# Ten propagation steps on TensorE: adjacency as weights, or y as weights

## The chip, the cores and the metric

The kernel runs on one core of a Trainium2 chip. The metric is the device time in microseconds (us) of one execution, from the first to the last instruction. Engines: PE (TensorE), DVE (VectorE), ACT (ScalarE), POOL (GpSimd), SP (SyncE, which here only issues DMAs).

## The reference

A graph network with four layers over 6250 nodes of 128 features and 100,000 edges, sorted by destination. Only the last layer is touched. It is a propagation over ten steps:

```python
norm = deg_inv_sqrt[src] * deg_inv_sqrt[dst]
def step(xk, _):
    msg = norm[:, None] * xk[src]
    agg = jax.ops.segment_sum(msg, dst, num_segments=n_nodes)
    return ((1.0 - ALPHA) * agg + ALPHA * h, None)
xK, _ = jax.lax.scan(step, x, None, length=10)
```

A step needs the whole result of the step before it: each node sums the rows of its sources.

## The kernel before

Nodes are padded to NT = 49 tiles of 128. In layer 3 the state C (f32) is kept in SBUF, scaled by the degrees, and called y. Each step sums y over the edges, for two kinds of destination tile:

- **Dense tiles**, the first DENSE = 38. Layer 0 has made the adjacency as a matrix of fp8 counts in DRAM (`adj`). A row of tiles of it, 128 partitions of 6272 bytes (784 KB), is loaded for each destination tile into one of six slots of `adj_ring` (`load_adj`, issued by SP once the tile that used the slot is multiplied).
- **Pooled tiles**, the last POOLED = 11. POOL gathers the y rows of their edges from DRAM, one indirect DMA per 128 edges (L988; 178 of them a step, in EGROUPS = 45 groups of up to EG = 4, in a ring `y_rows` of ERING = 5 groups); DVE makes one-hot rows (`step_hot`, L2793), and PE multiplies them (L1951).

y is held as two f16 halves side by side, an upper part and the rest (`halves(A)` in one step, `halves(E)` in the next, 256 columns per source tile). For a dense destination tile PE runs 49 matmuls (L1933): the weights are the 128x128 block of the adjacency, what moves is 128x256, both halves of one source tile. The sum of 49 stands in one of six PSUM banks, upper half in columns 0 to 127 and lower in 128 to 255, with destination nodes on the partitions.

DVE then works the tile off in four instructions: `w0` = C*sc_a + B (L2804, does not need the sum), `w1` = bank upper*sc_b + w0 (L2810), C = bank lower*sc_b + w1 (L2813, "y_tiles"), and after ACT has written the new upper half (L1416, "upper") the new lower half (L2821, "lower"). SP stores each tile's new y to DRAM (L733), into `table` or `x_spill` by turns, since POOL's gathers of the next step read it there. POOL starts a step's gathers only when all stores of the step before have landed ("y_out"), and each group only when PE is done with the group five before it ("edge_used").

Order: `step_plan` is one list, dense tile 0, 1, 2 and so on, with edge groups put between dense tiles so that they end with the last one: 45 groups among 38 tiles. `done_order` is the order in which tiles come out, and all engines follow it. The first dense tile of a step takes its 49 source tiles in `done_order` and waits for the last ones in stages (`LATE`). `settle` adds one semaphore instruction behind a wait. The ten steps are written as five calls of `two_steps`.

Of the kernel before, what the change touches and what calls it, by code (L numbers as in the profile page):

```python
# [15 lines left out]
P = 128  # L16
N_NODES, N_EDGES, D = 6250, 100000, 128
NT = (N_NODES + P - 1) // P
# [21 lines left out]
ADJ_SLOTS = 6  # L40
# [4 lines left out]
ADJ_PITCH = 1 << 13  # L45
SCALE = 1024.0
# [39 lines left out]
def build(nc, t, out):  # L86
    ctx = ExitStack()
    with ctx:
# [3 lines left out]
        def dram(name, shape, dt=F32):  # L92
# [7 lines left out]
                      "adj_in4": "dst_in0", "edge_hot0": "filter", "edge_used0": "filter_ps", "edge_rows0": "rows_in", "edge_rows1": "keys_in", "adj_in5": "y_stored", "y_out0": "spilled", "y_upper0": "seeds_in", "y_out1": "gat_back", "edge_used": "as_kept", "edge_hot_made": "x_free", "part_done": "step_link",  # L100
# [73 lines left out]
        adj_ring = arena[:, 0:ADJ_SLOTS * NP // 4].bitcast(F8).rearrange("p (s f) -> p s f", s=ADJ_SLOTS)  # L174
# [68 lines left out]

        y_rows = arena[:, ADJ_SLOTS * NP // 4:ADJ_SLOTS * NP // 4 + EG * ERING * D].rearrange("p (g k f) -> p g k f", k=EG, f=D)

# [27 lines left out]
        iota_y = w_gat[:, :].bitcast(BF16)  # L273
        bn_st, bn = sb("bn_st", [P, 14, 6]), sb("bn", [P, 4])
# [65 lines left out]
        step_plan, done_order = [], []  # L340
        for j in range(DENSE):
            step_plan.append(("dense", j))
            done_order.append(j)
            upto = min(EDGE_TILES, EG * (max(0, j - 1) * EGROUPS // (DENSE - 2)))
            for x in range(sum(kind == "edge" for kind, _ in step_plan), upto):
                step_plan.append(("edge", x))
                for i in range(DENSE, NT):
                    if near_last[i] == edge_first + x:
                        done_order.append(i)
        place = {i: p for p, i in enumerate(done_order)}  # L350

        LATE = {0: NT - 8, NT - 8: NT - 4, NT - 4: NT - 2, NT - 2: NT - 1, NT - 1: NT}
# [20 lines left out]
        def group_place(g):  # L373
            seen = 0
            for kind, x in step_plan:
                if kind == "edge" and x == g * EG:
                    return seen
                seen += kind == "dense" or any(near_last[i] == edge_first + x for i in range(DENSE, NT))

        hot_at = {}  # L380
        for g in range(EGROUPS):
            hot_at.setdefault(max(0, group_place(g) - 2), []).append(g)
        adj_loads = [len(range(u, DENSE, ADJ_SLOTS)) for u in range(ADJ_SLOTS)]
# [14 lines left out]
        step_banks = [ps[0][:, :], ps[1][:, :], ps[2][:, :], ps[3][:, :], pt[0][:, 0:512], pt[0][:, 512:1024]]  # L398
# [4 lines left out]

        def bank_of(i):
            return step_banks[i % ADJ_SLOTS] if i < DENSE else edge_banks[i % 2]
# [98 lines left out]
        def _(sp):  # L504
# [202 lines left out]
            def after_l2(b):  # L707
                if b == 0:
                    adj_r = adj.rearrange("(j p) b -> p j b", p=P)
                    ring_u8 = adj_ring.bitcast(U8)  # L710

                    def load_adj(u, j):
                        sp.dma_start(ring_u8[:, u:u + 1, :], adj_r[:, bass.ds(j, 1), 0:NP]).then_inc(sem(f"adj_in{u}"), 16)
                    sp.wait_ge(sem("ff2_ps"), ff_done[b > 0])
                    for u in range(ADJ_SLOTS):
                        load_adj(u, u)
# [6 lines left out]
                    def two_steps(pairs, last):  # L723
                        for half in range(2):
                            final = last and half == 1
                            to_v, new = ((spill_v, table_v)[half], nodes((A, E)[half]))

                            def keep_tile(p):
                                sp.wait_ge(sem("lower"), pairs * (2 * NT) + (half * NT + NT + p + 1))
                                settle(sp)  # L730
                                i = done_order[p]
                                if not final:
                                    sp.dma_start(to_v[:, i, :], new[:, i, :]).then_inc(sem(f"y_out{1 - half}"), 16)  # L733
                                elif i < FULL_TILES:
                                    sp.dma_start(out_v[:, i, :], nodes(X)[:, i, :]).then_inc(sem("out_stored"), 16)
                                else:
                                    sp.dma_start(out[i * P:N_NODES, :], nodes(X)[0:N_NODES - i * P, i, :]
                                                 ).then_inc(sem("out_stored"), 16)

                            for p, i in enumerate(done_order):  # L740
                                if i < (DENSE - ADJ_SLOTS if final else DENSE):
                                    sp.wait_ge(sem("multiplied"), pairs * (2 * NT) + (half * NT + p + 1))
                                    settle(sp)
                                    u = i % ADJ_SLOTS
                                    load_adj(u, i + ADJ_SLOTS if i + ADJ_SLOTS < DENSE else u)
                                if p:
                                    keep_tile(p - 1)
                            keep_tile(NT - 1)
# [2269 lines left out]
```

## Time and profile before

| | us |
|---|---|
| median of 3 runs | 6619.98 |
| lowest, highest | 6592.85, 6634.28 |
| span of the profiled execution | 6586.7 |
| PE busy in it | 4728.4 (72%) |
| POOL busy | 3399.2 (52%) |
| DVE busy | 2861.5 (43%) |
| ACT busy | 960.6 (15%) |

The profiled execution is 33 us under the median. Busy shares are averages over all layers; layer 3 is read in a stretch of its own. Matmuls overlap, so a busy PE is not one at its peak: the distance between starts says more. "Issue" is idle time for which the profile shows nothing that was waited for.

### The profile page before, as it was taken

The numbers are of one execution on the slowest core, as the hardware profiler recorded it, in microseconds if no ns is written. First come the engines' busy times: TensorE is split into PE (matmuls) and PEld (weight loads), VectorE is DVE, ScalarE is ACT, GpSimd is POOL, SyncE is SP. The second block draws the span as 40 slices with busy tenths as digits, with TensorE's granted clock in tenths as the row PEclk, the third lists the DMA queues.
The fourth block names the chain that finished last, engine by engine and source line by source line (L and its number), as shares of the span: only waits on it lengthen the run. The fifth ranks groups of instructions, "written<-read, shape, count | busy, mean of one in ns | idle before, by whom it ended". The sixth has DMA issues, their size and how long they took to land.

```text
span 6586.7 us, 89829 instructions
## 1 busy us (share of the span) xinstructions
PE 4728.4 (72%) x32959; PEld 3792.3 (58%) x32959; DVE 2861.5 (43%) x9191; ACT 960.6 (15%) x2766; POOL 3399.2 (52%) x3566
## 2 busy tenths in 40 slices
PE   3767468888762445555557888788888888888888
PEld 2655356555552344444445767667666666666666
DVE  6867434444433555555673323233333333233323
ACT  4656311111110000012130000000000000000000
POOL 3332456666545555555514555555555555555555
PEclk8888679898885666677778989899888898888989
DMA  5222212222212222222214444444444444444444
GB/s 129 79 80 72 77 51 56 56 56 56 55 44 71 68 70 74 74 68 64 69 48 148 152 142 150 144 145 154 145 148 145 148 150 149 144 149 145 153 144 124
DMA packets 366969, 690.33 MB, mean 105 GB/s; under 512 B 101617, under 2 KB 247703, under 8 KB 366512
## 3 DMA queue, kind: packets, MB, share of 16 engines
q1 hardware_dynamic: 246948, 445.91, 21.7%
q0 software_dynamic: 113216, 235.39, 13.8%
q8 instruction: 271, 4.44, 0.3%
q10 hardware_dynamic: 6364, 3.20, 0.2%
q14 instruction: 170, 1.39, 0.1%
HBM read 603.02 MB, written 81.51 MB: 104 GB/s over the span
## 4 chain that ended last, share of the span: by engine, by line
PE 51%; DVE 17%; another core or an unknown queue 16%; issue 12%; ACT 3%; DMA 0%; SPq 0%; POOL 0%; DVEq 0%; ACTq 0%
PE ps L1933 24%; PE pt L1933 11%; PE ps L1674 5%; PE pt L1951 4%; DVE E L2374 3%; DVE B L2454 2%; DVE arena L2496 1%; PE pt L2018 1%; DVE O L2937 1%; PE pt L1642 1%; PE ps L2009 1%; PE ps L1751 1%; ACT E L1484 1%; DVE scores L2933 1%
## 5 line engine op out<-in xcount | busy, mean ns | idle before, releaser
L988 POOL DMA_INDIRECT arena<-table,src_i x890 | 848.6, 953 | 824.2 <-PE pt L1951 293.7
L988 POOL DMA_INDIRECT arena<-x_spill,src_i x890 | 848.8, 954 | 699.8 <-PE pt L1951 273.7
L953 POOL DMA_INDIRECT E<-gat_table,src_i x782 | 760.2, 972 | 632.2 <-DVE arena L2496 364.9
L938 POOL DMA_INDIRECT arena<-table,src_i x782 | 742.9, 950 | 602.7 <-issue 217.4
L1674 PE MATMUL ps<-E,arena 128*128 128x352 f32 (+22 forms) x2932 | 788.7, 423 | 274.3 <-DVE E L2374 218.0
L1933 PE MATMUL ps<-E,arena 128*128 128x256 f16 x6370 | 822.7, 287 | 195.6 <-issue 163.6
L1933 PE MATMUL ps<-A,arena 128*128 128x256 f16 x6370 | 820.9, 286 | 163.6 <-issue 160.7
L1933 PEld LDWEIGHTS ps<-E,arena 128*128 128x128 fp8e4 x6370 | 647.2, 102 | 353.2 <-issue 255.1
L1933 PEld LDWEIGHTS ps<-A,arena 128*128 128x128 fp8e4 x6370 | 644.2, 102 | 318.3 <-issue 223.1
L1674 PEld LDWEIGHTS ps<-E,arena 128*128 128x128 f32 x2932 | 518.4, 212 | 476.4 <-DVE E L2374 259.4
L2810 DVE SCALAR_TENSOR_TENSOR O<-ps,sc_b,O 128x128 f32<-128x128 f32 x260 | 91.2, 351 | 1336.8 <-PE ps L1933 628.2
L1751 PE MATMUL ps<-arena,B 128*128 128x144 f32 x2244 | 510.4, 375 | 63.8 <-issue 63.3
L2374 DVE SCALAR_TENSOR_TENSOR E<-arena,pt 128x512 f32<-128x512 bf16 (+5 forms) x782 | 480.0, 674 | 161.0 <-remote 74.6
L1751 PEld LDWEIGHTS ps<-arena,B 128*128 128x128 f32 x2244 | 412.9, 249 | 80.7 <-issue 77.8
L1933 PE MATMUL pt<-E,arena 128*128 128x256 f16 x2940 | 363.2, 280 | 62.9 <-issue 62.1
L1933 PE MATMUL pt<-A,arena 128*128 128x256 f16 x2940 | 363.5, 281 | 54.5 <-issue 53.7
L1023 POOL DMA_INDIRECT A<-first_rows,src_i x178 | 178.5, 1003 | 357.0 <-PE pt L1993 253.8
L1933 PEld LDWEIGHTS pt<-E,arena 128*128 128x128 fp8e4 x2940 | 291.6, 100 | 122.0 <-issue 83.9
L1933 PEld LDWEIGHTS pt<-A,arena 128*128 128x128 fp8e4 x2940 | 293.9, 101 | 114.1 <-issue 74.2
L2018 PE MATMUL pt<-arena,E 128*128 128x258 f16 x1862 | 306.0, 287 | 63.6 <-ACT E L1484 38.6
L2810 DVE SCALAR_TENSOR_TENSOR O<-pt,sc_b,O 128x128 f32<-128x128 f32 x230 | 80.7, 351 | 589.4 <-PE pt L1933 316.3
L1484 ACT ACTIVATE E<-ps 128x490 fp8e4<-128x490 f32 (+1 forms) x494 | 291.2, 597 | 215.5 <-remote 141.7
(353 smaller groups left out, 5601.5 us busy)
## 6 DMA issues: line engine op xcount, KB each, us to landing
arena<-adj SPq DMA_DIRECT2D x380, 784.0 KB
adj<-E SPq DMA_DIRECT2D x38, 784.0 KB
arena<-table,src_i POOLq DMA_INDIRECT x1672
O<-dst_rows SPq DMA_DIRECT2D x112, 224.0 KB
x_spill<-A SPq DMA_DIRECT2D x245, 64.0 KB
arena<-x_spill,src_i POOLq DMA_INDIRECT x890
table<-E SPq DMA_DIRECT2D x196, 64.0 KB
E<-gat_table,src_i POOLq DMA_INDIRECT x782
```

The source lines that it names most:

```text
L938: pool.indirect_dma_start(out=rows_ring[:, k % RING, :], out_offset=None, in_=table, in_offset=bass.IndirectOffsetOnAxis(ap=src_i[:, k:k + ...
L953: pool.indirect_dma_start(out=att_rows[:, b % 3 * AB + at, :], out_offset=None, in_=gat_table, in_offset=bass.IndirectOffsetOnAxis(ap=src_ ...
L988: pool.indirect_dma_start(out=y_rows[:, g % ERING, k, :], out_offset=None, in_=(table, x_spill)[half], in_offset=bass.IndirectOffsetOnAxis ...
L1023: pool.indirect_dma_start(out=rows0[:, x % (2 * EG0), :], out_offset=None, in_=first_rows, in_offset=bass.IndirectOffsetOnAxis(ap=src_i[:, ...
L1484: act.activation(made[:, i % MADE, :, 2 * BD * q:2 * BD * q + w], ps[pair % 4][:, 0:w * NT].rearrange("p (d j) -> p j d", j=NT), ACT.Copy, ...
L1674: mm = pe.matmul(ps[m % 4][:, (lo - WD * m) * BASES:(hi - WD * m) * BASES], rows_ring[:, k % RING, :], m_ring[:, k % MS, lo - first_dst(k) ...
L1751: mm = pe.matmul(ps[i % 2][:, 0:WL2], edge_hot[:, (2 * b + half) % 3, k % AH, i % 2 * P:(i % 2 + 1) * P], weighted_rows[:, b % 2, k, :], s ...
L1933: mm = pe.matmul(bank_of(x)[:, 0:2 * D], adj_ring[:, u, i * P:(i + 1) * P], y[:, i, :], start=(p == 0), stop=(p == NT - 1))
L1951: mm = pe.matmul(bank_of(i)[:, 0:2 * D], step_hot[g % EHOT][:, k, i % 2 * P:(i % 2 + 1) * P], y_rows[:, g % ERING, k, :].bitcast(F16), sta ...
L2018: mm = pe.matmul(bank0_of(m)[:, 0:2 * LO], made[:, m % MADE, j, :], y16[:, j, :], start=(j == 0), stop=(j == NT - 1))
L2374: dve.scalar_tensor_tensor(m_ring[:, k % MS, w, :], bc(iota_h[:, w], BASES), dst_rel[:, k:k + 1], row_bc(made_c[:, c % 2, at, :], w.stop - ...
L2810: dve.scalar_tensor_tensor(w1, bank[:, 0:D], sc_b[:, tile:tile + 1], w0, MUL, ADD).then_inc(part_done, 1)
```

## The change

Layer 3 is turned around. The halves of y are the weights now, each 128x128 f16, and the adjacency moves: rows of one source tile for CHUNK = 4 destination tiles at once, 128x512 fp8 (the last chunk has 2 tiles). 38 dense tiles make ten chunks. Both halves of a source tile add into the same sum, so one bank holds four tiles, but with features on the partitions and nodes in the columns. ACT copies the bank to SBUF (`sums_in`), PE turns each tile back with a transpose (`turn_banks`), and DVE then needs one read of PSUM per dense tile, not two. Pooled tiles are computed as before.

The adjacency comes in pieces, four destination rows by 17 or 16 source tiles (rows of 2176 or 2048 bytes), thirty a step, in four slots. The plan of all ten steps is one sorted list: every dense matmul pair has a cost of two units (a full chunk 98, a step `LONG` = 931), a chunk's transposes come 10 units behind its end, its store 26 units; edge group g stands at 64 + 20 g, so the last of the 45 stands 13 units into the next step. Waits are on constants; the settles are gone except on POOL.

The diff, cut:

```diff
-ADJ_SLOTS = 6
+CHUNK, PARTS3, ADJ_RING = 4, [(0, 17), (17, 33), (33, 49)], 4
+PIECE = 17
+CHUNKS = (DENSE + CHUNK - 1) // CHUNK
+TURN_LAG, STORE_LAG, EDGE_LAG, EDGE_GAP = 10, 26, 64, 20
...
+        plan = []
+        for step in range(STEPS):
+            base = step * LONG
+            for c in range(CHUNKS):
+                for i in range(NT):
+                    plan.append((base + chunk_at_cost(c) + 2 * i * len(chunk_nodes(c)) / CHUNK, 0, "dense", step, c, i))
+                plan.append((base + chunk_at_cost(c + 1), -1, "copy", step, c, 0))
+                plan.append((base + chunk_at_cost(c + 1) + TURN_LAG, 1, "turn", step, c, 0))
+                plan.append((base + chunk_at_cost(c + 1) + STORE_LAG, 4, "store", step, c * CHUNK, chunk_nodes(c).stop))
+            for g in range(EGROUPS):
+                plan.append((base + EDGE_LAG + EDGE_GAP * g, 2, "edges", step, g, 0))
+                plan.append((base + EDGE_LAG + EDGE_GAP * g - 5 * EDGE_GAP // 2, 5, "hots", step, g, 0))
+            for i in range(DENSE, NT):
+                plan.append((base + EDGE_LAG + EDGE_GAP * pooled_group(i), 3, "pooled", step, i, 0))
+                plan.append((base + EDGE_LAG + EDGE_GAP * pooled_group(i) + STORE_LAG - TURN_LAG, 4, "store", step, i, i + 1))
+        plan = [entry[2:] for entry in sorted(plan, key=lambda entry: entry[:2])]
...
+        READ_UPTO = {0: 32, 32: 36, 36: NT - 1, NT - 1: NT}
...
# SP
-                        sp.dma_start(ring_u8[:, u:u + 1, :], adj_r[:, bass.ds(j, 1), 0:NP]).then_inc(sem(f"adj_in{u}"), 16)
+                        sp.dma_start(ring_u8[:, n % ADJ_RING, 0:len(some), 0:(last - first) * P],
+                                     adj_r[:, some.start:some.stop, first * P:last * P]
+                                     ).then_inc(sem(f"adj_in{n % ADJ_RING}"), 16)
...
# ACT
+                        if kind == "copy":
+                            n, w = step * CHUNKS + what, len(chunk_nodes(what)) * P
+                            act.wait_ge(sem("chunk_made"), n + 1)
+                            if n >= 2:
+                                act.wait_ge(sem("turned_out"), n - 1)
+                            act.activation(sums_in[:, n % 2, 0:w], chunk_banks[n % 2][:, 0:w], ACT.Copy
+                                           ).then_inc(sem("turn_in"), 1)
...
# PE
-                                        mm = pe.matmul(bank_of(x)[:, 0:2 * D], adj_ring[:, u, i * P:(i + 1) * P],
-                                                       y[:, i, :], start=(p == 0), stop=(p == NT - 1))
+                            for h in range(2):
+                                mm = pe.matmul(chunk_banks[n % 2][:, 0:len(some) * P], y[:, i, h * D:(h + 1) * D],
+                                               adj_ring[:, piece % ADJ_RING, 0:len(some), at:at + P],
+                                               start=(i == 0 and h == 0), stop=(i == NT - 1 and h == 1))
...
+                            for k in range(len(chunk_nodes(what))):
+                                mm = pe.transpose(turn_banks[n % 2][:, k * P:(k + 1) * P],
+                                                  sums_in[:, n % 2, k * P:(k + 1) * P], ident[:, :])
+                            mm.then_inc(sem("turned_out"), 1)
...
# DVE
+                            for k, i in enumerate(chunk_nodes(what)):
+                                kept_of(k, i)
+                            dve.wait_ge(part_done, parts[0])
+                            dve.wait_ge(sem("turned_out"), n + 1)
+                            for k, i in enumerate(chunk_nodes(what)):
+                                dve.scalar_tensor_tensor(nodes(C)[:, i, :], turn_banks[n % 2][:, k * P:(k + 1) * P],
+                                                         sc_b[:, i:i + 1], kept_part[:, k, :], MUL, ADD
+                                                         ).then_inc(sem("y_tiles"), 1)
+                            for i in chunk_nodes(what):
+                                lower_of(step, i)
```

## Rows read from the trace of the kernel before

**Rows 1.** The page's slices: PE busy in tenths, and GB/s, 40 equal slices.

```profile
PE   3767468888762445555557888788888888888888
GB/s 129 79 80 72 77 51 56 56 56 56 55 44 71 68 70 74 74 68 64 69 48 148 152 142 150 144 145 154 145 148 145 148 150 149 144 149 145 153 144 124
```

**Rows 2.** Stretches: busy us (instructions) of each engine, clock, DMA share, GB/s.

```profile
4101.40:4410.70 309.30, 258.30 (x2100) 210.22 (x2099) 97.34 (x374) 15.15 (x49) 169.47 (x178) 0.91 0.48 148
5340.00:5650.00 310.00, 260.69 (x2096) 211.26 (x2094) 97.21 (x374) 15.15 (x49) 169.96 (x178) 0.89 0.48 148
```

**Rows 3.** Groups of one step, 4101.4 to 4410.7 (busy, mean | idle before, releasers).

```profile
L1933 PE MATMUL ps<-E,arena 128*128 128x256 f16 x1274 | 164.2, 286 | 36.9 <-issue 36.4
L1933 PE MATMUL pt<-E,arena 128*128 128x256 f16 x588 | 70.1, 277 | 7.3 <-issue 6.9
L1951 PE MATMUL pt<-arena,rows 128*128 128x256 f16 x150 | 22.4, 286 | 5.3 <-issue 5.3
L1951 PE MATMUL pt<-arena,weight_e 128*128 128x256 f16 x44 | 6.9, 272 | 1.6 <-issue 1.6
L1951 PE MATMUL pt<-arena,rel_i 128*128 128x256 f16 x44 | 6.6, 273 | 0.0
...
L2810 DVE SCALAR_TENSOR_TENSOR O<-ps,sc_b,O 128x128 f32<-128x128 f32 x26 | 9.1, 351 | 140.9 <-remote 69.4 <-PE ps L1933 60.4 <-PE pt L1951 11.1
```

**Rows 4.** Timeline of PE and its loads over one dense tile (start, us).

```profile
4404.61 5.34 PEld L1933 LDWEIGHTS ps<-E,arena 128*128 128x128 fp8e4 x49
4404.72 5.51 PE L1933 MATMUL ps<-E,arena 128*128 128x256 f16 x49
...
4410.07 0.60 PE L1951 MATMUL pt<-arena,weight_e 128*128 128x256 f16 x4
```

**Rows 5.** Stretches in runs of POOL's gathers (columns as rows 2).

```profile
4108.20:4115.80 7.60, 7.60 (x72) 6.83 (x70) 1.57 (x7) 0.00 (x0) 5.76 (x6) 1.00 0.40 140
4116.00:4133.10 17.10, 4.82 (x17) 1.46 (x15) 1.61 (x7) 0.31 (x1) 13.06 (x14) 0.64 0.37 105
...
4145.70:4152.30 6.60, 6.60 (x63) 5.93 (x61) 2.78 (x12) 0.03 (x1) 3.91 (x4) 1.00 0.50 166
4158.90:4166.40 7.50, 7.50 (x71) 6.74 (x69) 1.21 (x5) 0.31 (x1) 5.68 (x6) 1.00 0.52 155
...
4262.30:4274.30 12.00, 6.12 (x31) 3.21 (x30) 1.66 (x7) 0.31 (x1) 5.68 (x6) 0.71 0.33 86
```

**Rows 6.** Timeline of POOL (start, us; in brackets the idle time before).

```profile
4132.08 0.95 POOL L988 DMA_INDIRECT arena<-table,src_i  x1 [0.30 <-issue]
...
4158.97 0.95 POOL L988 DMA_INDIRECT arena<-table,src_i  x1 [1.82 <-PE pt L1951]
...
4167.73 0.94 POOL L988 DMA_INDIRECT arena<-table,src_i  x1 [0.30 <-issue]
```

**Rows 7.** Timeline of PE where it comes back to full pace.

```profile
4136.58 0.61 PE L1951 MATMUL pt<-arena,rows 128*128 128x256 f16 x2 [0.30 <-issue]
...
4170.43 2.12 PE L1933 MATMUL ps<-E,arena 128*128 128x256 f16 x18 [0.48 <-issue]
```

**Rows 8.** A stretch of layer 2 with fourteen gathers (columns as rows 2).

```profile
2490.60:2508.20 17.60, 11.36 (x72) 10.26 (x72) 10.62 (x28) 0.00 (x0) 13.40 (x14) 0.75 0.36 93
```

**Rows 9.** Timeline of PE in that stretch.

```profile
2501.24 0.42 PE L1817 MATMUL pt<-ident,E 128*128 128x128 f32 x1
2501.45 0.42 PE L1818 MATMUL pt<-ident,E 128*128 128x128 f32 x1
...
2506.21 0.28 PE L1751 MATMUL ps<-arena,B 128*128 128x144 f32 x1 [1.51 <-issue]
```

**Rows 10.** A group of the page: ACT reading PSUM.

```profile
L1484 ACT ACTIVATE E<-ps 128x490 fp8e4<-128x490 f32 (+1 forms) x494 | 291.2, 597 | 215.5 <-remote 141.7
```

**Rows 11.** Timeline at a step's end: last edge products, first gather.

```profile
4410.51 0.38 PE L1951 MATMUL pt<-arena,rows 128*128 128x256 f16 x2
...
4417.32 0.95 POOL L988 DMA_INDIRECT arena<-x_spill,src_i  x1 [22.69 <-DMA x_spill<-A]
```

## What the change should do to the time

> **What bounds the kernel now.** I read the slices of the page first. Layer 3 is the stretch from slice 21 on, where DMA moves 142 to 154 GB/s, and it takes nearly half of the span. PE is busy in 7 to 8 tenths there [rows 1]. A table by step then shows ten equal steps: one takes 309.3 us, with some 2,100 matmuls, 178 gathers on POOL and a granted clock of 0.91 [rows 2]. Then the groups of that step. DVE's idle time is ended by PE or a remote queue, so PE sets the pace; the reader should see that what ends PE's own idle time is "issue", 36.4 + 6.9 + 5.3 + 1.6 = 50 us of it [rows 3]. PE waits for no data that the profile knows. It runs 38 x 49 = 1862 dense matmuls and, by the same rows, 238 edge ones (two of them the next step's: 2098 in all).
>
> What would the step be without these holes? A dense tile with none has its 49 matmuls between 4404.72 and 4410.07: 109.2 ns for 256 columns [rows 4]. 2098 x 0.1092 = 229.1 us. The step is 309.3, so 80 us are lost. Where? The holes have a pattern that is best seen by laying POOL's timeline beside PE's:
> - From 4108.2 to 4133.0 POOL issues 20 gathers. PE runs 72 matmuls and 70 loads in the first 7.6 us, and then 17 matmuls and 15 loads in the next 17.1 us [rows 5]. POOL's last gather of this run ends at 4133.0 [rows 6], and PE is back at 4136.6, 3.6 us later [rows 7].
> - From 4145.7 four gathers and a pause of 1.8 us: 63 matmuls in 6.6 us, nothing lost [rows 5].
> - From 4158.97 eight gathers, 1.25 us apart, to 4168.7 [rows 6]: 71 matmuls in 7.5 us [rows 5], then a hole, and PE is back at 4170.4 [rows 7], 1.7 us after the last gather: 4 us. The run of twelve from 4254.8 leaves 31 matmuls in the 12 us from 4262.3 [rows 5]: 9 us lost.
>
> So while POOL gathers without a pause, PE is fed from a store that holds so much, and is refilled at 32 instructions in 17.1 us, 1.9 per us. The store is 142 - 7.6 x 1.9 = 128 instructions. Is it a count or a time (7.6 us)? Layer 2 tells: there PE is slower (72 matmuls in 17.6 us, [rows 8]), and 14 gathers from 2490.7 open no hole before 2504.7, 14 us in, after about 70 matmuls [rows 9]. It is a count: 140 - 14 x 1.9 = 113 instructions by this row.
>
> In the step this makes one hole of 20 us, some seven of 4 us and two or three of 9 us, less the matmuls done in them: 65 us. The other 15 us are matmuls at the lower level of the clock, 1.2 instead of 2.4 GHz, which follows the long holes: the clock stands at 0.64 and 0.71 in these, against 1.00 in whole stretches [rows 5].
>
> **The change part by part.**
> *Dense matmuls.* 1862 of 256 columns become 2 x 49 x 10 = 980: 882 of 512 columns and 98 of 256. The columns are the same 476,672. By the 109.2 ns of [rows 4], 256 columns at 2.4 GHz are 106.7 and 2.5 is left for each instruction, so 512 cost 215.8 ns: 882 x 0.2158 + 98 x 0.1092 = 201.0 us, against 203.3 now. Halving the weight loads gives nothing by itself: a load of 98 ns lies beside every one of those matmuls, and the 109.2 ns hold no room for it [rows 4]. No row shows fp8 as the moving operand; bounds are 201 and, if the columns went at the clock's lower level, 402; I take 201, since in the rows 128x256 f16 goes at a column per cycle.
>
> The Trainium skill, "TensorE: Matmul & The Clock Gate", LDWEIGHTS section, puts a load at its columns over 1.2 (107 ns) and Part 3 says that one overlaps a running matmul only if its row group differs. By that rule 882 loads saved would be worth 94 us a step. The trace disagrees: a pair takes 109.2 ns in all.
>
> *Edges:* the same 236, 25.8 us. *Transposes back:* 38 a step, f32, ident as partner. Two such transposes start 0.21 us apart [rows 9]: 8.0 us, new on PE. PE unbroken: 201.0 + 25.8 + 8.0 = 234.8 us, 6 more than now.
> *ACT:* ten copies of 128x512 at about 0.6 us (one of 490 columns: 0.6, [rows 10]) and the 49 activations: 21 us, hidden. *DVE:* one read of PSUM fewer for 38 tiles, -13 us (38 x 0.351, [rows 3]) of 97; hidden. If the chain turn, copy, DVE came late, PE has two chunk banks, 21 us each; no cost.
> *The adjacency loads:* 30 of 1.1 MB for 38 of 784 KB, rows of 2176 bytes for 6272, four slots. A piece is used in 34 x 0.216 = 7.3 us and asked for three pieces, 22 us, ahead; DMA's share is 0.48 now [rows 2]. With three times the packets the share is bounded by 0.48 and, should time go by packets, 1.4. Layer 2, whose gathers move short rows, has 93 GB/s at a share of 0.36, 258 at a full one, against 308 here [rows 2, 8]; so I take 0.6. Cost 0. SP is in order: a store waiting for "lower" holds the next load by 6 us at most, inside the 22.
> *The settles* (one semaphore instruction behind a wait on PE and SP) go. Nothing: at full pace PE shows no hole where they stand.
> *Instructions of PE:* 2 x (980 + 236 + 38) = 2508 a step for 4196.
>
> *The gathers* stay: 178 x 1.25 = 222.6 us of POOL, 5.0 us per group of four [rows 6]. But their place against PE changes, and this decides. Now a group comes between dense tiles of 5.35 us, mostly one, so that POOL pauses 1.8 us after four gathers. The new plan has a group every 20 units: 20 x 0.2158, 5.3 edge matmuls and 0.9 transposes are 5.07 us, as long as the gathers themselves, and a released POOL starts 0.9 us late, so it never pauses by itself. PE takes 52 instructions in 5.07 us, 10.3 per us, so the store shrinks at 8.4 per us and lasts 128 / 8.4 = 15.2 us (13.4 by layer 2's 113), twice as long as now.
>
> One step, from its first dense matmul:
> 1. The last group stands 13 units into the step. From PE's last edge product to POOL's first gather are 6.6 us now (4410.7 to 4417.3, [rows 11]). POOL starts at 9, group 0 has landed at 16.2 where PE wants it at 14.5: 2 us lost.
> 2. PE does groups 0, 1, 2 by 26.4, and the store is empty there. The ring holds five groups ahead, so POOL runs eight groups, until 49, and PE is back after about 54.5 (the delay after the last gather grows with the run: 1.7 us at 8, 3.6 at 20; I take 5.5 at 32). In 28 us PE does 27 matmuls at 17.1/17 us each, 5.4 us of work. Lost so far: 54.5 - 30 = 24.5 us, against 18 for the same hole now.
> 3. Now the ring is full. PE's groups x, +5.07, +10.1 and +15.2 release POOL, which starts at x + 0.9 and ends at x + 20.9; the store is empty at x + 16.1; PE is back at x + 23.8 with 7 matmuls done and does the next group at x + 26.6. Four groups in 26.6 for 20.3 us: 1.6 us lost per group. With the smaller store only three groups fit: 18.2 for 15.2, 1.0 per group. Mean 1.3, from group 3 to 39: 36 x 1.3 = 47 us (36 to 57). Then POOL is done with the step and PE runs free.
> 4. Lower clock: 15 us now. Holes fewer but longer: 15 again, 5 to 28 as bounds.
>
> Sum: 234.8 + 24.5 + 47 + 15 = 321 us a step, against 309.3: +12 a step, +120 in ten. The profiled execution's span is 6586.7 us, the median of the three runs 33 above it, so 6707 by the span and 6740 as a median. What surrounds layer 3 stays.
>
> **The rivals.**
> - *A count that just shrinks (faster).* The holes go with PE's instructions: 65 x 2508/4196 = 39 us, the clock's 15 to 9, 234.8 + 39 + 9 = 283 a step: 6350 as median. For it: the store is a count, and each instruction works twice as long. Against: POOL's pauses are gone. It decides from the point where POOL pauses 0.8 us or more about every third group, which irregular edge groups could give.
> - *No holes at all.* If 15 us of store always meet a pause, PE takes 234.8 + 2, and POOL 222.6 + 9: 240 a step, 5920. Nothing but that store speaks for it; the first run of gathers alone speaks against.
> - *The store is a time, not a count (slower).* Then PE starves 7.6 us into any run: 27.5 us in the first hole, two groups in 13.4 for 10.1 us after that, 38 x 1.65 = 63; 234.8 + 27.5 + 63 + 15 = 340, 6920. Layer 2 speaks against it [rows 8, 9]. The Trainium skill, "Runtime: NRT & Kernel Launch", Instruction fetch mechanics, has each engine's instructions streamed in 16 KiB blocks, mostly hidden, so that their number would not matter and this rival would stand; the trace has holes that it does not explain.
> - *The loads come late.* If 2176-byte rows take the packets' time of 6272, PE waits for adjacency: up to 340, 6920.
> - *The turn pays on loads:* 94 us less than now, 224, stopped by POOL at 232: 5840. [rows 4] exclude it nearly.
>
> **How the numbers follow.** Forecast 0.48, its own range 6600 to 6880; the shrinking count 0.26; no holes 0.08, with the loads' gain 0.01; time 0.08; late loads 0.09. Faster by over 1%, about what a measurement of this kernel can tell, is a step under 303: the second, third and last cases and little of the forecast's (its low end is 300): 0.37. Within 1%, 303 to 317: 0.38 of the forecast's, 0.18. Slower: 0.45. The range reaches from 6300, which takes the shrinking count in, to 6900.
>
> **What would show it.** Dense matmuls 216 ns apart in whole stretches (else the 201 is wrong); "issue" still the one reason of PE's idle time, 45 to 80 us a step; holes that open some 70 matmuls after POOL's start and close 2 to 4 us after its last gather; POOL in runs of 30 or more at the step's start and 12 to 16 after, not 4. Idle time put down to DMA would be the late loads; a step with no holes breaks the forecast.

## The result, and the profile after

| us | before | after |
|---|---|---|
| median of 4 runs | 6609.43 | 6390.7 |
| lowest, highest | 6592.85, 6634.28 | 6368.28, 6407.98 |
| span of the profiled execution | 6586.7 | 6377.2 |

The ratio is 0.9678, with an interval of [0.9634, 0.9723]: 3.2% faster. The forecast was 6740, 1.8% slower. The time lies in the range, but on the other side of no change.

The slices of the page of after: PE busy and the granted clock in tenths, and GB/s. They answer to [rows 1].

```profile
PE   3756568888874444455545888898988788798888
PEclk9878788888886666667767999899999899899999
GB/s 133 77 66 77 78 55 53 53 57 55 56 58 59 66 71 69 64 74 65 70 70 60 155 156 164 150 172 151 161 161 163 153 154 166 149 165 152 164 157 141
```

Stretches of three whole steps of after (start and end in us, length, then busy us and instructions of PE, PEld, DVE, ACT and POOL, granted clock, DMA share, GB/s). They answer to [rows 2].

```profile
4072.60:4357.20 284.60, 243.75 (x1257) 125.88 (x1255) 78.81 (x336) 19.54 (x59) 170.99 (x178) 0.93 0.52 160
4357.20:4642.40 285.20, 243.70 (x1256) 125.41 (x1254) 78.46 (x336) 19.42 (x59) 172.25 (x178) 0.94 0.52 160
5221.60:5509.40 287.80, 245.91 (x1256) 125.38 (x1254) 78.56 (x336) 19.54 (x59) 172.34 (x178) 0.92 0.51 158
```

A step takes 284.6 us where it took 309.3. The mean over the ten is 286.6 for 310.1: layer 3 gains 235 us in the profiled execution, and so holds all of the gain (its span is 209.5 shorter; layer 3 starts at 3502.5 us for 3477.2, and in the runs e4 to e8 between 3470 and 3507). PE has 1,257 matmuls for 2,100, DVE 78.8 us for 97.3, POOL its 178 gathers as before, and the DMA share went from 0.48 to 0.52 only.

Groups of PE in the step from 4072.6 (busy, mean ns | idle before, and what ended it), and its timeline in a whole stretch (start, us, operation, count):

```profile
L1950 PE MATMUL ps<-arena,E 128*128 128x512 fp8e4 (+1 forms) x980 | 218.8, 376 | 8.2 <-issue 8.1
L1962 PE MATMUL ps<-ident,O 128*128 128x128 f32 x38 | 7.3, 324 | 31.3 <-ACT O L1438 25.8 <-issue 5.5
...
3712.07 0.60 PE L1962 MATMUL ps<-ident,O 128*128 128x128 f32 x4
3712.50 1.89 PE L1950 MATMUL ps<-arena,E 128*128 128x512 fp8e4 x8
3714.99 4.48 PE L1950 MATMUL ps<-arena,E 128*128 128x512 fp8e4 x20
3719.31 0.93 PE L1980 MATMUL pt<-arena,rows 128*128 128x256 f16 x7
```

At full pace 20 dense matmuls take 4.32 us (3714.99 to 3719.31), 216.0 ns each for 512 columns, and four transposes 0.43 us. New is an idle time that ACT's copy ends: 25.8 us at L1962.

### The profile page after: what moved, and what is told of

Read it like the earlier page. It is cut to its first block, busy times and chain, and to the rows that moved or that the text cites. A ratio compares the mean times of both kernels' runs of the same rounds, so it can differ in the third digit from the quotient of the medians.

```text
span 6377.2 us, 70089 instructions
## 1 busy us (share of the span) xinstructions
PE 4557.4 (71%) x24519; PEld 2925.3 (46%) x24519; DVE 2668.5 (42%) x8811; ACT 1003.7 (16%) x2866; POOL 3558.0 (56%) x3566
## 3 DMA queue, kind: packets, MB, share of 16 engines
q0 software_dynamic: 113216, 235.39, 14.3%
## 4 chain that ended last, share of the span: by engine, by line
PE 42%; another core or an unknown queue 27%; DVE 18%; issue 10%; ACT 2%; POOL 1%; DMA 0%; ACTq 0%; DVEq 0%; SPq 0%
PE ps L1950 25%; PE ps L1697 5%; PE pt L1980 3%; DVE E L2399 3%; DVE B L2479 2%; PE pt L2043 2%; PE ps L1774 2%; DVE arena L2521 1%; PE pt L1665 1%; DVE O L2975 1%; PE ps L2034 1%; PE ps L1962 1%; POOL A L1038 1%; DVE arena L2502 1%
## 5 line engine op out<-in xcount | busy, mean ns | idle before, releaser
L1950 PE MATMUL ps<-arena,E 128*128 128x512 fp8e4 (+1 forms) x4900 | 1101.9, 377 | 84.7 <-issue 53.4
L1950 PE MATMUL ps<-arena,A 128*128 128x512 fp8e4 (+1 forms) x4900 | 1102.2, 377 | 48.3 <-issue 46.2
L1950 PEld LDWEIGHTS ps<-arena,E 128*128 128x128 f16 x4900 | 486.5, 100 | 599.6 <-issue 156.6
L1950 PEld LDWEIGHTS ps<-arena,A 128*128 128x128 f16 x4900 | 486.8, 100 | 560.8 <-issue 116.8
L2847 DVE SCALAR_TENSOR_TENSOR C<-ps,sc_b,scores 128x128 f32<-128x128 f32 x380 | 107.5, 345 | 920.6 <-PE ps L1962 656.5
L1038 POOL DMA_INDIRECT A<-first_rows,src_i x178 | 312.7, 1757 | 258.6 <-PE pt L2018 155.8
L2860 DVE SCALAR_TENSOR_TENSOR scores<-pt,sc_b,scores 128x128 f32<-128x128 f32 x110 | 38.6, 351 | 711.5 <-remote 480.9
L2975 DVE TENSOR_SCALAR O<-arena 128x245 bf16<-128x245 bf16 x988 | 231.6, 317 | 175.0 <-issue 64.4
L1962 PE MATMUL ps<-ident,O 128*128 128x128 f32 x380 | 69.6, 311 | 281.7 <-ACT O L1438 257.6
L2034 PE MATMUL ps<-O,scores 128*128 128x245 bf16 x988 | 197.2, 283 | 94.3 <-ACT E L1507 73.3
```

The source lines that it names most:

```text
L1038: pool.indirect_dma_start(out=rows0[:, x % (2 * EG0), :], out_offset=None, in_=first_rows, in_offset=bass.IndirectOffsetOnAxis(ap=src_i[:, ...
L1950: mm = pe.matmul(chunk_banks[n % 2][:, 0:len(some) * P], y[:, i, h * D:(h + 1) * D], adj_ring[:, piece % ADJ_RING, 0:len(some), at:at + P] ...
L2034: pe.matmul(ps[pair % 4][:, h * BW:(h + 1) * BW], hot_src[:, g % SRC, :], hot_code[:, g % HOT, 0:BW], start=True, stop=True).then_inc(sem( ...
L2975: dve.tensor_scalar(hot_code[:, g % HOT, 0:BW], iota_w[:, 0:BW], slot_c[:, g // P, g % P:g % P + 1], None, ALU.is_equal).then_inc(sem("hot ...
```

## Where a step's time is

By those paces PE's unbroken work is 201 (dense) + 25.8 (edges) + 38 x 0.108 = 4.1 (transposes) = 231 us. The other 53.6 of the 284.6 are 1.2 us at the start (PE waits for the first gathered rows), one long hole of 22.1, and 30.3 in the rest of the step. The hole, from both engines' timelines:

```profile
4072.59 2.75 PE L1950 MATMUL ps<-arena,E 128*128 128x512 fp8e4 x12
4081.25 0.99 POOL L1003 DMA_INDIRECT arena<-table,src_i  x1 [23.46 <-DMA table<-E]
4087.66 0.61 PE L1980 MATMUL pt<-arena,rows 128*128 128x256 f16 x4 [0.22 <-DMA arena<-table,src_i]
4093.64 4.48 PE L1950 MATMUL ps<-arena,E 128*128 128x512 fp8e4 x20
4097.96 0.60 PE L1980 MATMUL pt<-arena,rel_i 128*128 128x256 f16 x4
4099.57 0.38 PE L1950 MATMUL ps<-arena,E 128*128 128x512 fp8e4 x1 [0.33 <-issue]
...
4115.12 0.95 POOL L1003 DMA_INDIRECT arena<-table,src_i  x1 [0.30 <-issue]
4120.62 0.36 SPq L734 DMA_DIRECT2D arena<-adj  x1
4120.62 0.60 ACT L1438 ACTIVATE O<-ps 128x512 f32<-128x512 f32 x1 [42.15 <-remote]
4121.27 1.11 PE L1962 MATMUL ps<-ident,O 128*128 128x128 f32 x4 [21.32 <-ACT O L1438]
4121.50 0.95 POOL L1003 DMA_INDIRECT arena<-table,src_i  x1 [5.43 <-remote]
```

Chunk 0's last matmul ran at 4096.0. Three engines wait on what PE counted up around then: ACT for its copy, SP for the next load, POOL for the group of 4098. All three go on between 4120.6 and 4121.5, some 4.5 us after the last of 28 gathers ends (4116.1). So the semaphores that PE raises while POOL gathers without a pause arrive up to 24 us late. PE then waits for ACT's copy, which puts "ACT" where "issue" stood before; the late semaphore and the stop of PE come in the same stretch (whether the wait for ACT costs anything of its own is tested by e8).

The holes after that are small. Stretches of after, each run of twelve gathers followed by its pause:

```profile
4099.90:4121.20 21.30, 0.06 (x1) 0.00 (x0) 0.00 (x0) 0.58 (x1) 12.29 (x13) 0.54 0.16 43
...
4271.70:4286.00 14.30, 14.30 (x75) 7.17 (x74) 5.56 (x26) 0.97 (x4) 10.95 (x12) 1.00 0.69 217
4286.00:4289.40 3.40, 2.00 (x10) 0.74 (x8) 0.73 (x4) 0.54 (x1) 0.53 (x1) 1.00 0.13 34
4289.40:4304.30 14.90, 14.90 (x82) 7.91 (x80) 4.83 (x20) 1.15 (x5) 11.45 (x12) 1.00 0.68 212
4304.30:4307.10 2.80, 1.61 (x8) 0.52 (x6) 1.89 (x10) 0.31 (x1) 0.03 (x1) 1.00 0.18 50
```

From 4271.7 on, 75 matmuls with 74 loads go at full pace over 14.3 us, and from 4289.4 on 82 with 80 over 14.9; only then comes a hole of about 2 us. Before, 72 matmuls lasted 7.6 us [rows 5]. 149 instructions less 14.3 x 1.9 of refill are 122; 162 less 14.9 x 1.9 are 134. The forecast's store was 128.

POOL's pauses are late news too. Its group that starts at 4289.41 waits for edge products that PE ended at 4281.5:

```profile
4280.89 0.60 PE L1980 MATMUL pt<-arena,rel_i 128*128 128x256 f16 x4
4285.58 0.95 POOL L1003 DMA_INDIRECT arena<-table,src_i  x1 [0.31 <-issue]
4289.41 0.95 POOL L1003 DMA_INDIRECT arena<-table,src_i  x1 [2.89 <-remote]
...
L1003 POOL DMA_INDIRECT arena<-table,src_i x178 | 171.0, 961 | 115.4 <-issue 54.2 <-remote 25.3 <-DMA table<-E 23.5
```

Of the 149 pauses of over 0.6 us within ten steps, 134 begin when PE is already done with the group that POOL waits for, and in these POOL goes on 6.5 us (median) after PE was done. Right behind the long hole it goes on 0.8 us after.

Worked out over all ten steps from the starts of matmuls and gathers (a pause is over 0.6 us; lost is the median of the time of a run with its pause, less its matmuls at full pace, so the lower clock is in it):

| gathers in a run | after: a step has | run + pause, us | lost each, us | before: a step has | lost each, us |
|---|---|---|---|---|---|
| 28 (before 20) | 1 | 40.2 | 23.5 | 1 | 20.2 |
| 16 | 2.1 | 23.6 | 5.6 | none | |
| 12 (before 11, 12) | 6.4 | 17.8 | 2.2 | 2.4 | 8.1 to 9.5 |
| 8 | 2.3 | 11.8 | 0 | 7.1 | 3.6 |
| 4 | 2.7 | 6.9 | 1.7 | 16.6 | 0 |

(The runs of 4 in after are mostly those right behind the long hole, at the lower clock.) So the change lost POOL's short pauses and still gained: a run of 12 costs 2.2 us now and cost 9 before. In a run of 8 in before, PE makes 67 matmuls in 7.7 us until the first hole; in a run of 12 now it is 75 in 15.2 (medians).

## The experiments

Two theories stand against each other at first. By the count theory PE holds some 128 instructions ahead, and the turn pays because each of them does twice the work. By the rival the gain comes from elsewhere: less work of PE or DVE, or the settles gone. The open question behind both is why POOL's runs end after 12 gathers. Each ratio is to the runs of before of its own session, with a 95% interval. Steps from here on are means of the eight between the first and the last; counted so, after has 287.5 and before 310.3.

**No runs of gathers.** Of each group's four gathers only the first is made, and PE multiplies its rows in place of the others; three quarters of the gathers are left out. In after and in before:

```diff
-for k in range(group_size(g)):
+for k in range(1):
...
-y_rows[:, r, k, :].bitcast(F16),
+y_rows[:, r, 0, :].bitcast(F16),
```

> The changed kernel with one gather of each group of four (the other three are left out; PE multiplies the first one's rows four times), so POOL never gathers for more than 1.3 us at a stretch. All matmuls, loads, transposes and adjacency loads stay. Theory (PE loses its time behind POOL's runs of gathers): no holes, clock near 1.00 in layer 3, a step at PE's unbroken 230 to 237 us against 286 now, whole kernel 5850 to 5920 us. Rival (the holes are PE's own instruction supply or the adjacency loads): a step of 275 us or more, 6260 us or more.

> The same cut in the kernel before: one gather of each group of four, the other three left out. Theory: a step at its unbroken 229 to 233 us against 310, whole kernel 5770 to 5840 us, so that with no runs of gathers the change gains nothing and costs 0 to 60 us. Rival (the change gains by itself on PE): the changed kernel stays ahead by 100 us or more when both are cut like this.

Measured: 5829.8 and 5792.6 us (one run each), steps of 231.0 and 229.1. One step of each:

```profile
4209.30:4440.30 231.00, 231.00 (x1256) 123.40 (x1254) 78.37 (x337) 19.41 (x59) 42.74 (x45) 1.00 0.51 160
...
4184.50:4413.70 229.20, 229.20 (x2102) 205.43 (x2100) 97.26 (x375) 15.15 (x49) 42.97 (x45) 1.00 0.51 161
```

No hole is left in either, and the clock is at 1.00. Without the runs of gathers the turn is 37 us slower, and not faster. All that it gains goes with the gathers, and adjacency in rows of 2176 bytes costs next to nothing. The edit takes the gathers' transfers out as well as their runs. That the run counts, and not the traffic, is in the table above: four gathers and a pause lost nothing in before, twenty lost 20 us.

**As many instructions as before.** The turned layer with chunks of two tiles, so that dense matmuls move 256 columns again; lags in units are doubled and so the same in time.

```diff
-CHUNK, PARTS3, ADJ_RING = 4, [(0, 17), (17, 33), (33, 49)], 4
+CHUNK, PARTS3, ADJ_RING = 2, [(0, 17), (17, 33), (33, 49)], 6
-TURN_LAG, STORE_LAG, EDGE_LAG, EDGE_GAP = 10, 26, 64, 20
+TURN_LAG, STORE_LAG, EDGE_LAG, EDGE_GAP = 20, 52, 128, 40
```

> The changed kernel with two destination tiles in a chunk instead of four: the matmuls are 1862 of 256 columns again, as many PE instructions as before, all else turned around as in the change (lags doubled in units, six slots of half the size). Theory (the gain comes from half the PE instructions while POOL gathers): PE is stopped after some 70 matmuls, 7.6 us into a run, and the gain is gone: a step of 300 to 330 us, 6520 to 6820 us. Rival (the gain is in the turned form itself, the plan or the missing settles): it keeps its 286 us step, 6350 to 6420 us.

```profile
4106.50:4416.10 309.60, 259.44 (x2139) 215.00 (x2137) 81.56 (x336) 21.37 (x68) 169.57 (x178) 0.92 0.53 148
```

Measured: 6579.0, ratio 0.997 [0.9948, 0.9992], a step of 308.6. The gain is gone with the number of instructions, though the settles, DVE's reads and the plan are as in after. In its runs of 8 the first hole comes after 68 matmuls, 7.6 us in (medians of 113), as in before, and such a run loses 3.6 us. The edit also makes the pieces and ACT's copies smaller and twice as many, but in its step from 4096.4 only 1.4 us of PE's idle time is put down to DMA and 2.7 to ACT's copies. That settles the count theory against the rival. Whether matmuls are counted or instructions can't be told here, since each matmul has its load.

**Ending POOL's runs sooner.** Three ways: POOL waits for a group two later; or it waits after each three groups for its own last gather to land; or it fills 1000 unused columns and waits for that, after each two or three groups.

```diff
-pool.wait_ge(sem("edge_used"), pairs * (2 * EGROUPS) + (half * EGROUPS + g + 1))
+pool.wait_ge(sem("edge_used"), pairs * (2 * EGROUPS) + (half * EGROUPS + g + 1 + 2))
```

> The changed kernel with POOL let only three groups ahead of PE instead of five (it waits for two more groups of PE). Theory: the first run of a step is 12 gathers and not 28, so the 22 us hole at the step's start shrinks to 2 to 5 us; runs after it are at most 12. A step of 262 to 275 us, 6150 to 6270 us. Rival (less lead makes PE wait for landed gathers): PE idle for the gathers' DMA, a step of 286 us or more.

```diff
+if g and g % 3 == 0:
+    q = g - 1
+    pool.wait_ge(y_in[q % ERING], <all gathers up to group q landed>)
```

> The changed kernel; after every third group POOL waits until its own last gathers have landed (some 2 us) before it starts the next group. No other edit. Theory (PE is stopped by runs of gathers, and a pause sets it free): no run longer than 12, the 28-gather run and its 22 us hole gone; POOL needs 222.6 + 14 x 2 + 9 = 260 us a step, PE 231 plus small holes: a step of 262 to 275, 6140 to 6270 us. Rival (the step is held by POOL's rate alone): more waiting of POOL makes it slower, 290 us or more a step.

```diff
+if g and g % 2 == 0:        # e7: g % 3
...
+    pool.memset(arena[:, 11300:12300], 0.0).then_inc(sem("paused"), 1)
+    pool.wait_ge(sem("paused"), paused[0])
```

> The changed kernel; after every second group POOL fills 1000 columns of an unused part of SBUF and waits for that, so that it pauses, but for nothing that PE or a DMA does. Theory: no run over 8 gathers (9.7 us), less than the 15 us that PE's store lasts, so no holes but a few; POOL needs 222.6 + 22 x 1.5 + 9 = 265 us a step at a pause of 1.5 us: 262 to 272 us, 6130 to 6240 us, and PE's clock near 1.00. Rival (a pause must be a wait on PE or a DMA to help): holes as before, 290 us or more.

> As the run before, with the pause after every third group: runs of 12 gathers, 14.8 us, where the store lasts some 15. Theory: POOL needs 222.6 + 14 x 1.5 + 9 = 253 us, but now and then the store is empty just before the pause, 1 to 3 us each: 258 to 272 us a step, 6090 to 6230 us. If a pause of 1.5 us does not set PE free: 275 or more.

| | us | ratio | step | runs in ten steps |
|---|---|---|---|---|
| e4, two groups less ahead | 6316.3 | 0.9568 [0.9532, 0.9605] | 280.8 | 88 of 12; the first 16 |
| e5, own landing, 12 gathers | 6381.5 | 0.9677 [0.9649, 0.9705] | 287.7 | 116 of 12 |
| e6, a fill, 8 gathers | 6333.4 | 0.9607 [0.9581, 0.9633] | 283.3 | 201 of 8 |
| e7, a fill, 12 gathers | 6364.9 | 0.965 [0.961, 0.9689] | 286.8 | 96 of 12 |

All four missed what was expected of them (between 258 and 275). The pauses came as planned; the timelines of POOL and PE in e5 show why they do not pay (in brackets POOL's idle time):

```profile
4103.32 0.94 POOL L1007 DMA_INDIRECT arena<-table,src_i  x1 [0.30 <-issue]
4105.68 0.37 PE L1984 MATMUL pt<-arena,rows 128*128 128x256 f16 x1 [1.02 <-issue]
4106.39 1.68 PE L1984 MATMUL pt<-arena,rows 128*128 128x256 f16 x7 [0.34 <-issue]
4106.65 0.96 POOL L1007 DMA_INDIRECT arena<-table,src_i  x1 [2.38 <-remote]
```

The run ends at 4104.26, and PE is at full pace at 4106.39, 2.1 us later. POOL starts again at 4106.65: of its pause of 2.4 us PE had 0.3. Over the runs of after, PE comes back 1.2 us after 4 gathers, 1.7 after 8, 2.3 after 12, 3.6 after 20 and 5.2 after 28, about 0.5 + 0.155 n for a run of n. A pause shorter than that refills nothing: 1.8 us after 8, as in e6, is worth 0.1. What had been expected took each pause for whole. e4 gains 1.1% on after, by the two ratios. Its first run is of 16 gathers, not 28, and that loses 6.8 us, not 23.5; but PE still waits 9.6 us for ACT's copies in a step, and 8.8 runs of 12 a step lose 2.9 us each.

**Is it the waiting transpose?** In the long hole PE stood before the transposes of chunk 0. Here these, with their stores, come 60 units later (part of the last step is then worked off with a value not made yet, which changes the output, not the work).

```diff
+def turn_lag(c):
+    return 70 if c == 0 else TURN_LAG
```

> The changed kernel, with the transposes of the first chunk of each step (and their stores) 60 units later in the plan, all else the same. In the changed kernel PE stands 21 us before these transposes, for ACT's copy, whose semaphore came late. Theory (PE's own store of outgoing events is full anyway then): PE goes on some matmuls at the slow pace, 0 to 5 us gained per step, 6340 to 6400 us. Rival (it only waits for the late semaphore and could work on): 12 us or more per step gained, 6270 us or less.

Measured: 6370.4, 0.9658 [0.9626, 0.9689], a step of 286.3 for 287.5 in after. Freed from the wait, PE makes nine matmuls between 4088.9 and 4108.1, with "issue" as the only reason of its idle time. The hole is PE's own; the wait for ACT lies in its shadow, within some 1 us a step.

**Fewer gathers.** Eight pooled tiles and not eleven: 130 gathers a step, three more dense tiles; in after (with the groups 29 units apart), in before, and with e4's wait on top.

```diff
-POOLED = 11
+POOLED = 8
-TURN_LAG, STORE_LAG, EDGE_LAG, EDGE_GAP = 10, 26, 64, 20
+TURN_LAG, STORE_LAG, EDGE_LAG, EDGE_GAP = 10, 26, 64, 29
```

> The changed kernel with 8 pooled tiles instead of 11 (41 dense; some 130 gathers in 33 groups a step; edge groups 29 units apart instead of 20, so that the last one ends as before with the step). Theory (a run of n gathers holds PE's events for 1.25 n us and some 0.5 + 0.15 n more, and a longer pause than that sets it free): a group now comes every 7 us for 5 us of gathers, so POOL pauses 2 us after each four, more than the 1.2 us needed, and the holes go but for the step's first run. PE unbroken 240 us, step 250 to 262 us; three more dense tiles in layer 0 cost 30 us: 6040 to 6180 us. Rival (holes come with PE's work, not with POOL's runs): a step of 290 us or more, as PE has 9 us more to do.

> The same number of pooled tiles, 8, in the kernel before. Theory: 33 groups among 41 dense tiles, so no two in a row and no runs of 8; left are the 20 us hole of the first run and its clock: PE unbroken 41 x 49 x 0.1092 + 19 = 238 us, step 262 to 272 us, 6140 to 6280 us, so that the change is worth less than 150 us here. Rival (the turned form is better by itself): 200 us or more behind the changed kernel with 8.

> Both: 8 pooled tiles and POOL at most three groups ahead, in the changed kernel. Theory: the first run is 12 to 16 gathers, its hole of 22 us shrinks to some 5, later runs are 4 anyway: step 244 to 252 us, 5980 to 6100 us. Rival (the hole at the step's start is PE's wait for the first stores and not for POOL's run): no gain over five groups ahead.

> The kernel before with POOL at most three groups ahead. Theory: the first run falls from 20 gathers to 12, its hole from 20 us to some 9, and runs of 12 later go: a step of 295 to 304 us against 310, 6440 to 6540 us. Rival (holes do not depend on the run's length): within 1% of the kernel before.

| | us | ratio | step |
|---|---|---|---|
| e9, after with 8 pooled | 6101.8 | 0.9216 [0.9178, 0.9255] | 261.0 |
| e10, before with 8 pooled | 6271.9 | 0.9463 [0.9416, 0.951] | 277.3 |
| e11, e9 with e4's wait | 5972.0 | 0.902 [0.8978, 0.9063] | 249.2 |
| e12, before with e4's wait | 6587.7 | 0.9933 [0.9903, 0.9963] | 307.0 |

A step of e11, and POOL in it:

```profile
4230.50:4478.30 247.80, 241.33 (x1286) 122.57 (x1285) 67.44 (x284) 19.78 (x60) 123.74 (x129) 0.99 0.58 180
...
4012.91 0.95 POOL L1003 DMA_INDIRECT arena<-table,src_i  x1 [0.31 <-issue]
4015.63 0.95 POOL L1003 DMA_INDIRECT arena<-table,src_i  x1 [1.78 <-PE pt L1980]
```

Three more dense tiles cost PE work (1,286 matmuls for 1,257), and still the step of e11 falls by 38 us: groups 29 units apart leave a pause after nearly each four gathers (240 runs of 4 in ten steps), and the clock stands at 0.99. e11 is the best version found, 10% under before and 6.8% under after by the two ratios. The first edit is not worth more after the turn than before it: it takes 33 us off a step of before (e10) and 26.5 off one of after (e9). The turned kernel stays ahead by 16 us a step, 170 in all, where under 150 had been expected by the theory and 200 or more by the rival.

Each edit alone in before missed what was expected (e10: 277.3 for 262 to 272; e12: 307.0 for 295 to 304). Its store is used up 7.6 us into a run [rows 5], so that e10's 41 runs of 8 in ten steps still cost 4.4 us each and its ten runs of 20 cost 20.8. e12 has no runs of 20, but 4.1 of 12 a step at 9.7 us each, for 2.4 in before. Both edits together were not run in before, so how much of e11's gain needs the turn is open.

**What fills the store?** Dense matmuls carry few semaphore increments. Either increments that wait to be delivered fill a queue of some length and stop PE (A), or only instructions count (B). Here every dense matmul increments.

```diff
+if not (h == 1 and (i == NT - 1 or i + 1 == PARTS3[r][1])):
+    mm.then_inc(sem("spare"), 1)
```

> The changed kernel with a semaphore increment, which nobody waits for, on every dense matmul that had none. No instruction is added. Theory A (PE's outgoing events wait in a store of some 130 places, and each increment takes one, as each matmul and load does): three places per matmul for two, so that PE is stopped after some 45 to 50 matmuls, 10 us into a run, not 70 to 80 and 15; a step of 300 to 340 us against 287, 6520 to 6900 us. Theory B (only instructions or their records count): PE is stopped after 70 to 80 matmuls as before, 285 to 290 us a step, 6360 to 6420 us.

Measured: 5091.5, with before at 5063.0 (5047.7 to 5078.9 in six runs) in the same session: ratio 1.0068 [1.0035, 1.01]. Before is 23% faster in that session than in the others, and this kernel 20% faster than when it was run again (e16). A step of e13, and its page's PE and clock slices:

```profile
4134.60:4371.00 236.40, 232.51 (x1257) 122.86 (x1256) 79.20 (x339) 19.42 (x59) 169.18 (x178) 1.00 0.61 193
...
PE   3999589999884566566667999999999999999999
PEclk9999689999986676787778999999999999999999
```

POOL makes all 178 gathers of a step in one run of 223 us, PE keeps its full pace through it, and PE's semaphores arrive in time. The mean step is 237.9; the rival with no holes had 240. The layers ahead gain even more: layer 3 starts at 2703 us here and at 3478 in e16, the same kernel. The holes, then, are not in the program alone: they were in five sessions and missing in this one. Of before only the times are known from it; they fit steps of some 235 us, if what precedes them took as long as here (an estimate: 5063 less 2703, over ten). The question of A and B had to be asked again where holes are, beside repeats of after, before and e11:

> The changed kernel itself, on whatever chip this is. If the kernel before takes 6600 us here (a chip with holes): 6350 to 6430 us, 3% faster. If it takes 5060 us (a chip without): a step is bound by POOL and PE's unbroken 231 us, 234 to 240 us, against 229 to 236 before: 5050 to 5110 us, no faster and up to 1% slower.

> The kernel before itself, for its trace on this chip. With holes: steps of 310 us. Without: 49 dense matmuls 109 ns apart in every tile, a granted clock near 1.00 in layer 3, steps of 229 to 236 us.

> The changed kernel with an increment that nobody waits for on every dense matmul, again. On a chip with holes: theory A (an increment takes a place in PE's store) 45 to 50 matmuls to the first hole and 300 to 340 us a step; theory B (only instructions or their records count) 70 to 80 matmuls and 285 to 290 us a step. On a chip without: as e13, within 0.5% of the changed kernel.

> 8 pooled tiles and three groups ahead, again. With holes: 5970 us as in e11. Without: its gain was in the holes; PE's unbroken step is 240 us, 9 more than the changed kernel's, so 5120 to 5200 us, 1 to 3% slower than before.

| | us | ratio |
|---|---|---|
| e14, after (step 289.1) | 6377.9 | 0.967 [0.9635, 0.9706] |
| e15, before (step 309.2, one run) | 6588.5 | |
| e16, e13's kernel (step 291.3) | 6393.1 | 0.9692 [0.9666, 0.9719] |
| e17, e11's kernel (step 249.2) | 5965.7 | 0.9044 [0.8993, 0.9096] |

The holes are back. The expectations speak of a chip with holes and one without, but the record has the same chip number, 15, for e13 and, six minutes later, for these four runs. So, if that number names one chip, it is not a fixed property of the chip. With an increment on each of the 980 dense matmuls of a step, where some 30 had one, e16 is as after within the intervals, its step is 2 us longer than e14's where A had 13 or more, and its runs of 12 lose their pace after 73 matmuls (median), as in e14: B, though its step is 1 us above B's 285 to 290.

## Why the prediction was wrong

*Unbroken work: right.* 512 columns measure 216.0 ns (215.8 taken), so fp8 moves a column a cycle. The Trainium skill, "TensorE: Matmul & The Clock Gate", Back-to-back issue gap, has N/2.4 + 2.5 for an isolated matmul and 131 ns at 512 columns for a sustained stream; the trace agrees with the first, in a stream of 20. The transposes were over-sized: 0.21 us apart in layer 2 [rows 9], 0.108 here, 8.0 us became 4.1. That stretch of layer 2 had a clock of 0.75 [rows 8], and the granted clock was 0.50 from 2501.0 to 2501.9, where these two stand: a spacing at 1.2 GHz was taken for one at 2.4.

*The adjacency loads, ACT, DVE, settles at nothing: right.* With three quarters of the gathers gone both kernels come to their unbroken work (e1, e2), and the 25.8 us that PE waited for ACT are not ACT's (e8). No idle time of PE is put down to loads, the share is 0.52 (0.6 taken), DVE fell by 18.5 us for 13.

*The store is a count, and the turn doubles its time: right.* Forecast 128 instructions and a hole after 15.2 us; found 122 and 134, after 14.3 and 14.9. e3 takes the gain away by the count, and the rival in which the store is a time (6920) falls with it.

*Start and first hole: right, by two errors that cancel.* 24.5 us forecast, 1.2 + 22.1 measured. POOL's first run has 28 gathers, not 32, but PE does almost nothing in the hole (one matmul in 21.3 us), not 27.

*The steady holes: the step that failed.* Step 3 took 36 groups at 1.3 us, 47 us, and step 4 a further 15 for the clock: 62. Measured are 30.3 for both. Three things in it were wrong:
- *How long POOL's runs are, some 14 us.* The cycle was worked out with PE's credits reaching POOL at once, so that POOL goes on to 12 or 16 in every cycle and never pauses by itself. In the trace credits arrive late while POOL gathers, so POOL comes to its wait with its credit not there, and pauses (134 of 149 pauses). Only 2.1 runs of 16 are left in a step, and between them and the 6.4 of 12 lie 2.3 of 8, which lose nothing, and 2.7 of 4; half of the groups had been priced as runs of 16. At the forecast's own prices these counts give 6.4 x 3.0 + 2.1 x 6.4 = 33 us, not 47.
- *What a run costs, some 10 us.* Without the lower clock a run of 12 loses 1.6 us (3.0 forecast) and one of 16 loses 4.8 (6.4). Why they are cheaper is not shown.
- *The clock, some 7 us.* 15 us were kept from before. Measured are 8, from some 316 matmuls of 512 columns in ten steps at 427 ns, twice the 216, and 110 of 256 at 214; the same count in before gives 16. The lower level is granted for 40 us of a step where it was 66 before: as the rest has fewer holes, the clock falls less often.

With the clock in the prices, 6.4 x 2.2 + 2.1 x 5.6 + 2.7 x 1.7 = 30 us, and the sum ends at 231 + 23 + 30 = 284, the step that was measured.

*What in the rows of before told it.* DVE's wait for the sums of PE was ended by "remote" for 69.4 us [rows 3], and PE, which was back at 4136.6 [rows 7], had been waited for since before. I read these as PE being late. With what after shows they can also be read as news of PE being late, and a loop of credits between PE and POOL should have been worked out with that delay. That would have spoken for the rival of 283 us a step ("a count that just shrinks", 0.26), which came nearest: it decides where POOL pauses 0.8 us or more about every third group, and that is what happened, for a reason that I had not named for it (I had put it to irregular groups).

*Of the signs that were named*, runs of 30 or more and 12 to 16 after, POOL's were 28 and mostly 12, so these alone would not have told it; the holes behind them were smaller.

## What to carry to other kernels

When an engine stalls for no reason that the profile names, lay its timeline beside the others' and ask what it is a function of: here, how many instructions lie between two pauses of POOL. Instructions that each do more work are then worth more than their own time, though the same change is slightly slower where there is no stall (231.0 for 229.1). And before a loop of credits is worked out, look at how long a raised semaphore takes to be seen in the very state in which the loop runs; fewer gathers, further apart and with less lead (e11), took the gain from 3% to 10%. Part of that is not the turn's: the smaller number of gathers alone takes 5% off the kernel before (e10).

## What the hardware showed

- While POOL issues indirect DMAs 1.25 us apart, PE gets on for some 120 to 135 instructions and then nearly stops; its semaphores reach other engines late by as much as 24 us. It resumes 0.5 + 0.155 n us after a run of n. The Trainium skill, "TensorE: Matmul & The Clock Gate", Architectural detail, gives PE a queue of 64 instructions; the trace has twice as many run on. The Trainium skill, "Runtime: NRT & Kernel Launch", Instruction fetch mechanics, has the fetch mostly hidden; the runs here do not show whether the fetch or something else is behind the stop.
- One session of six had none of it: before 5063 us for 6591 to 6624, and the one kernel that was traced there has no holes in its steps. The gathers of layer 3 had the same pace there (223 us for 178), and the record has the same chip number for a session with the holes six minutes later. Why is open.
- Also open: whether the stop exists without a profile being taken (every timed run here carries spans and clocks), and the ratio of after itself in such a session. Only the kernel with more increments was timed there, 0.7% slower than before, which goes with e1 against e2 (0.6%).
